# Values in self-attention: the low and high parts of three query tiles in one product of 129 columns, put together by VectorE

## The reference, cut to what matters

```python
q = (xq @ wq).reshape(b, sq, H, DH).transpose(0, 2, 1, 3)      # k and v likewise
scores = jnp.einsum('bhqd,bhkd->bhqk', q, k) / math.sqrt(DH)
attn = jax.nn.softmax(scores, axis=-1)
out = jnp.einsum('bhqk,bhkd->bhqd', attn, v)
```

## Time and profile before

| | |
|---|---|
| median of 3 runs | 1155.06 us (1154.7 to 1155.65) |
| the profiled execution's own time | 1157.49 us |
| its span | 1155.7 us |
| PE busy | 1075.3 us (93%), 12759 instructions |
| PE weight loads | 688.0 us (60%), 12766 |
| DVE busy | 820.2 us (71%), 1364 |
| ACT busy | 617.2 us (53%), 1123 |
| POOL busy | 699.0 us (60%), 640 |
| granted clock of PE, mean | 0.985 |

### The profile page before, as it was taken

The page is one execution under the profiler, slowest core; times in us unless marked ns, Lnnn a source line. Parts: engine busy times, 40 slices in busy tenths (PEclk is TensorE's granted clock), DMA queues, the critical chain, the costliest instruction groups (busy, mean ns, idle before and its releaser), DMA issues.

```text
span 1155.7 us, 30603 instructions
## 1 busy us (share of the span) xinstructions
PE 1075.3 (93%) x12759; PEld 688.0 (60%) x12766; DVE 820.2 (71%) x1364; ACT 617.2 (53%) x1123; POOL 699.0 (60%) x640
## 2 busy tenths in 40 slices
PE   6999998999999999999999998989899979999986
PEld 3555555565665665665656655567667656665654
DVE  5686876846756667867757567668778767797786
ACT  4456565545455455555555455544444543267677
POOL 6586887866566577867766665446436634434333
PEclk9899999999999999999999999999999999999997
DMA  9422021121120120220220222123533352000001
GB/s 310 115 56 56 3 56 31 27 56 30 30 56 16 42 57 1 57 56 2 57 56 2 56 56 75 31 61 70 143 72 77 73 160 71 1 1 10 15 14 38
DMA packets 35818, 63.52 MB, mean 55 GB/s; under 512 B 10985, under 2 KB 22689, under 8 KB 33441
## 3 DMA queue, kind: packets, MB, share of 16 engines
q1 hardware_dynamic: 34373, 60.90, 21.0%
q10 hardware_dynamic: 1308, 0.66, 0.2%
HBM read 20.62 MB, written 2.10 MB: 20 GB/s over the span
## 4 chain that ended last, share of the span: by engine, by line
PE 64%; DVE 20%; DMA 7%; ACT 4%; issue 3%; POOL 1%; SPq 1%; ACTq 0%; DVEq 0%; POOLq 0%
PE outs L827 9%; DVE neg_max L1909 8%; PE scores L901 8%; PE scores L902 7%; PE scores L962 5%; DMA head_operands<-neg_max_rows 4%; PE outs L976 4%; PE outs L923 3%; PE outs L925 3%; PE outs L924 3%; PE outs L799 3%; PE outs L839 3%; PE scores L799 2%; PE mixed L856 2%; PE scores L827 1%
## 5 line engine op out<-in xcount | busy, mean ns | idle before, releaser
L1619 POOL TENSOR_TENSOR exps_rest<-exps 128x1024 f16<-128x1024 f32 (+1 forms) x297 | 513.9, 1736 | 271.6 <-ACT exps L1262 269.6
L1262 ACT ACTIVATE exps<-scores 128x512 f32<-128x512 f32 (+1 forms) x576 | 328.8, 595 | 276.4 <-PE scores L902 258.6
L923 PE MATMUL outs<-values,exps 128*128 128x65 f16 (+1 forms) x2176 | 227.2, 193 | 5.4 <-DVE attn_out L1937 4.5
L901 PE MATMUL scores<-head_operands 128*128 128x512 f16 (+1 forms) x576 | 219.9, 382 | 11.2 <-DMA head_operands<-neg_max_rows 8.3
L924 PE MATMUL outs<-values,exps 128*128 128x64 f16 (+1 forms) x2176 | 227.1, 192 | 0.0
L925 PE MATMUL outs<-values,exps_rest 128*128 128x65 f16 (+1 forms) x2176 | 226.7, 195 | 0.0
L923 PEld LDWEIGHTS outs<-values,exps 128*128 128x128 bf16 (+1 forms) x2176 | 201.6, 98 | 40.4 <-issue 12.8
L902 PE MATMUL scores<-head_operands 128*128 128x512 f16 (+1 forms) x576 | 219.2, 381 | 0.0
L924 PEld LDWEIGHTS outs<-values,exps 128*128 128x128 bf16 (+1 forms) x2176 | 200.9, 98 | 21.9
L925 PEld LDWEIGHTS outs<-values,exps_rest 128*128 128x128 f16 (+1 forms) x2176 | 200.9, 97 | 0.0
L1909 DVE TENSOR_REDUCE neg_max<-mixed 128x1 f32<-128x1024 f32 x128 | 156.0, 1219 | 34.1 <-PE mixed L857 32.5
(11 more groups left out here) (220 smaller groups left out, 1885.0 us busy)
## 6 DMA issues: line engine op xcount, KB each, us to landing
head_operands<-qk_pairs SPq DMA_DIRECT2D x65, 256.0 KB, 3.2
head_operands<-qk_pairs SPq DMA_DIRECT2D x31, 512.0 KB, 5.7
head_operands<-qk_pairs SPq DMA_DIRECT2D x34, 128.0 KB, 2.5
stage<-in_L_xcond_ff_w_dram SPq DMA_DIRECT2D x3, 1024.0 KB, 5.6
residual<-in_x_dram SPq DMA_DIRECT2D x4, 512.0 KB, 9.9
stage<-in_L_ffn_w_dram SPq DMA_DIRECT2D x2, 1024.0 KB, 5.1
head_operands<-in_x_dram SPq DMA_DIRECT2D x1, 2048.0 KB, 8.3
out_dram<-head_operands SPq DMA_DIRECT2D x16, 128.0 KB, 1.7
```

What stands on the lines that cost most here:

```text
L901: mm(o, kb[:, KH, :], hb[:, QS, :], start=True, stop=False)
L923: mm(o, eb[:, sl], vb[:, DH:VW], start=(kt == 0 and q == 0), stop=False, skip_group_check=True)
L1262: A(E[0:a.ks, c % RING, j * HALF:(j + 1) * HALF], score_bank(a, c, j), ACT.Exp, scale=SCALE).then_inc(s.exps, 1)
L1619: G.tensor_tensor(R[0:a.ks, c % RING, 0:n], e, e.bitcast(BF16).rearrange("p (n two) -> p n two", two=2)[:, :, 1], ALU.subtract).then_inc(s ...
```

## The change

For query tiles 1 to 3 of a chunk, the products at L923 and L924 become one of 129 columns: low values, high values, ones. The bank `outs0` then holds 65 columns for query tile 0, which stays as it was, and 129 columns for each of the other three (452 of 512). The product with the rests stays at 65 columns and adds into the high part and the ones.

DVE then has five instructions in place of two: the reciprocal (of four values 129 columns apart), the multiply of tile 0 (64 columns, a tensor_scalar), the multiply of the three high parts (192 columns), the multiply of the three low parts (192 columns, into the new tile `low_parts`), and, after a wait for the latter, the sum of the two in SBUF (192 columns). The semaphore `emptied` rises after the multiply of the low parts, `summed` after the sum. PE's values steps of self-attention wait for `emptied` where they waited for `summed`; the "out" items still wait for `summed`. Cross-attention stays as it was.

```diff
+        lows = sb("low_parts", [P, 2, TPH - 1, DH], F32)
...
-                if gr == 0:
-                    pe.wait_ge(s.summed, CREDIT + 4 * g + h * 2 + half - (a.kt == 1))
+                if gr == 0 and ai == 0:
+                    at_least(pe, s.emptied, 4 * g + h * 2 + half)
+                elif gr == 0:
+                    pe.wait_ge(s.summed, CREDIT + 4 * g + h * 2 + half - 1)
...
                 for q in range(TPH):
-                    o = outs(a, c)[:, q * (DH + 1):(q + 1) * (DH + 1)]
+                    wide = ai == 0 and q > 0
+                    o = outs(a, c)[:, q * VW - DH:q * VW + DH + 1] if wide else outs(a, c)[:, q * (DH + 1):(q + 1) * (DH + 1)]
                     for j in range(a.kpc):
...
-                        mm(o, eb[:, sl], vb[:, DH:VW], start=(kt == 0 and q == 0), stop=False, skip_group_check=True)
-                        mm(o[:, 0:DH], eb[:, sl], vb[:, 0:DH], start=False, stop=False, skip_group_check=True)
-                        last = mm(o, R[0:a.ks, slot, sl], vb[:, DH:VW], start=False, stop=(kt == a.kt - 1),
+                        if wide:
+                            mm(o, eb[:, sl], vb[:, 0:VW], start=False, stop=False, skip_group_check=True)
+                        else:
+                            mm(o, eb[:, sl], vb[:, DH:VW], start=(kt == 0 and q == 0), stop=False, skip_group_check=True)
+                            mm(o[:, 0:DH], eb[:, sl], vb[:, 0:DH], start=False, stop=False, skip_group_check=True)
+                        last = mm(o[:, DH:VW] if wide else o, R[0:a.ks, slot, sl], vb[:, DH:VW], start=False, stop=(kt == a.kt - 1),
...
+                if ai == 0:
+                    n = 4 * g + 2 * h + half
+                    low = outs(a, c)[:, DH + 1:DH + 1 + 3 * VW].rearrange("p (t c) -> p t c", c=VW)
+                    dst = Osb[:, half * TPH:(half + 1) * TPH, h * DH:(h + 1) * DH]
+                    V.reciprocal(rden[:, half, :], outs(a, c)[:, DH:DH + 3 * VW + 1:VW]).then_inc(s.recip, 1)
+                    dve.wait_ge(s.recip, n + 1)
+                    V.tensor_scalar(dst[:, 0, :], outs(a, c)[:, 0:DH], rden[:, half, 0:1], None, ALU.mult)
+                    V.tensor_tensor(dst[:, 1:TPH, :], low[:, :, DH:2 * DH],
+                                    rden[:, half, 1:TPH].unsqueeze(2).to_broadcast([P, TPH - 1, DH]), ALU.mult)
+                    V.tensor_tensor(lows[:, n % 2, :, :], low[:, :, 0:DH],
+                                    rden[:, half, 1:TPH].unsqueeze(2).to_broadcast([P, TPH - 1, DH]),
+                                    ALU.mult).then_inc(s.emptied, 1)
+                    dve.wait_ge(s.emptied, n + 1)
+                    V.tensor_tensor(dst[:, 1:TPH, :], dst[:, 1:TPH, :], lows[:, n % 2, :, :], ALU.add).then_inc(s.summed, 1)
+                    return
```

More of the change, by code:

```diff
@@ L536, in __init__ @@
                 s.recip = sem(n + "_recip")
-                s.summed = sem(n + "_summed")
+                s.summed, s.emptied = sem(n + "_summed"), sem(n + "_emptied")
                 s.qk_hi, s.qk = sem(n + "_qk_hi"), sem(n + "_qk")
```

## The result

The changed kernel takes 1214.27 us (median of 3 runs, 1212.58 to 1215.41) against 1155.06: a ratio of 1.0507, with a 95% interval of 1.049 to 1.0525. It is 59.2 us slower. The forecast was 46.7 us slower, 1201.8 us, and the measured time lies 1.3 us above the upper end of the range. The direction and most of the places were right. One cost was not in the sum at all.

The account below looks back on a forecast made before the run. The prediction took a chain of waits alternating between PE and DVE as the bound. Terms 34.6 + 10.5 + 5.2 + 1.4 = 51.7 us, less 5 on PE, gave 46.7 us slower: 1201.8 us, range 1175 to 1213.

Parts of the forecast that it names:

- The sums after values 15: PE's transposes wait for these sums; DVE's sum, held up by POOL, was to cost 34.6 us over 16 units.
- 13 units x 2.48 = 32.2: After values 15, units 1 to 13: the sum ends 2.48 us later than the old multiply, 32.2 us together.
- The race of the two starts: After values 15, POOL's rest starts 0.05 us before DVE's sum; rival, sum first: 1179.8 us, chance 0.24.
- 2.48 - 0.79: After values 15, delay per unit: 2.48 us if POOL starts first, 0.79 if the sum does.
- DVE's durations: Multiplies of 192 at 356 ns, one tile's at 273, sum alone 0.36 us; sum ready 0.86 after the old multiply's start.
- After values 7: Sum ends 1.39 us later: 5.6 us in units 8 to 11, 4.9 in units 0 to 3, hidden elsewhere.
- After values 11: PE waits for the bank 0.40 us longer in units 4 to 15 and unit 1: 5.2 us.
- One of the rivals: Dearer still: DVE's rest after values 11 behind POOL in units 8 to 11, or values 7 unhidden; 1213 us, chance 0.08.
- After values 3: DVE's idle 1.8 us or more covers the 1.4 us delay; only unit 0 pays 1.4 us.
- PE: Values steps: one 129-column product replaces two, saving 5.4 ns each, 8.3 us in all, 5 us on the chain.
- The 81 ns: Rival for PE's wide product: the page's price makes it dearer than the two replaced; some 1225 us, chance 0.01.
- PE's wait before the transposes: PE's total wait for DVE there, 7.9 us before the change, was to be near 40 us.

Follow-up runs that it names:

- idle products: Changed kernel plus ten 512-column products before PE's wait for the sums after values 15, units 1 to 7, 12, 13: 1201.97 us, both times run.
- narrow products: Changed kernel with DVE's five instructions on the old 65- and 64-column products, three tiles' result doubled: 1218.92 us, ratio 1.0556.
- measured alone: Kernel before with the 129-column products only, low parts of three tiles left out of the result: 1152.65 us, ratio 0.9968.
- race lost everywhere: Changed kernel with one more 64-column multiply before the sums after values 15 in units 8 to 11: 1224.89 us, ratio 1.0609.
- tile 0 last: Changed kernel with tile 0's multiply moved behind those of three tiles, just before the sum: 1188.09 us, ratio 1.0277.

## Why the prediction was wrong

The ruler splits the loss of the profiled executions in four. In the middle is what the forecast's terms give for each part, at right the changed kernel and the one with idle products (its second profile, with nine lost units), each minus before. Parts end at the reciprocal after values 15.

| part of the span | forecast | after | idle products |
|---|---|---|---|
| to unit 0's last sum | 2.2 | 2.4 | 2.7 |
| from there to unit 13's | 40.3 | 47.1 | 32.5 |
| from there to unit 15's | 3.5 | 6.7 | 5.1 |
| behind it, with cross-attention | 0.8 | -1.1 | -5.0 |
| sum | 46.8 | 55.1 | 35.3 |

In the second row both measured numbers are 1.6 us too small for what the change costs: between values 3 and 7 of unit 7 the profile before is longer than all the others by about that much.

- **The step that failed** is "The sums after values 15", in "13 units x 2.48 = 32.2", which prices PE's longer wait by its length and nothing else. The length was right (2.39 us in unit 4). What it left out is that PE's clock, at 1.00 from unit 1 to unit 13 before, falls to 0.50 behind each of the nine waits of 3 us: 14.6 us over eight laps and 1.6 behind unit 13, some 16 us in the profiles compared here, 10 between the medians of the two kernels run side by side. The kernel before had PE idle for at most 0.8 us at this place. But one part of its trace did show the price, and I hadn't read it, unit 14, by windows:

```profile
714.00:717.00 3.00, 1.28 (x25) 0.68 (x21) 3.00 (x4) 0.52 (x1) 2.15 (x1) 0.97 0.47 111
717.00:718.00 1.00, 1.00 (x17) 0.78 (x16) 1.00 (x2) 0.00 (x0) 0.00 (x0) 0.50 1.08 376
718.00:719.00 1.00, 1.00 (x16) 0.67 (x13) 0.60 (x3) 0.00 (x0) 0.00 (x0) 0.50 0.91 321
```

  PE has 1.28 us of work in 3 us, and then works at 0.50. A forecast that makes PE idle for 3 us once a unit has to ask what such a place costs.
- **The race of the two starts** was rightly named as the hinge, but it is not one answer for all units. I had POOL first by 0.05 us in 13 units. It was in nine; in units 8 to 11 the sum was first by 0.04. The step took the reciprocal's place from before's rows, right behind DVE's maximum; in these four units the maximum is over by then, and the reciprocal starts 0.10 us sooner against POOL. Each of those saved 2.48 - 0.79 = 1.69, together 6.8 us, so this error went the other way and hid part of the first. With nine lost units the forecast for unit 0 to 13 is 33.5 us, and the kernel with idle products, which has nine and no low clock, shows 32.5 (34.1 with the 1.6 us of unit 7 added). A single execution doesn't settle the count: of the four profiles with wide products and this order of instructions three have nine, and one, with idle products, has 11; the one on narrow products has ten.
- **DVE's durations** were right: 348 ns for 356 forecast, 284 for 273, 0.36 for the sum alone, 1.06 us from the reciprocal to the sum.
- **After values 7**: 1.39 us forecast in units 8 to 11. There the ruler grows by 1.24 between values 7 and 11, the wide products' gain included. In units 0 to 3 it grows by 0.85 to 1.28, where 1.1 to 1.4 was forecast. Hidden in units 4 to 7, 12 and 13, as forecast, but not in unit 14 (1.8 us) and unit 15 (0.3).
- **After values 11**: 0.40 forecast, with 0.10 off for the products; units 4 to 7, 12 and 13 have +0.31 or +0.32, but unit 1 has +0.74 and units 8 to 11 have +0.53 to +0.83. One of the rivals had a delay in units 8 to 11 at this place; I did not trace what it is. **After values 3**: hidden, as forecast, but for unit 0, where 1.4 was forecast and the ruler grows by 1.38 to values 7.
- **PE**: 5 us forecast, 3.7 measured alone. The 81 ns of the Trainium skill, "TensorE: Matmul & The Clock Gate", section "Back-to-back issue gap", did not show: the trace has 57.7 ns from a product of 129 columns to the next. With the rests' product behind it that makes 86.9 ns, where three products took 92.4: 5.5 saved for the 5.4 forecast.
- **PE's wait before the transposes**: forecast near 40 us, 35.6 with nine units lost and 42.7 with 13.

Not explained: 55.1 us is the difference of two executions, 59.2 that of the medians. The last part of the table differs by 4 us between the two kernels, though nothing in it was changed; I have not traced that.

## What to carry to other kernels

Price a longer wait of TensorE twice, once by its length and once by what the clock does behind it: here a wait that went from 0.5 to 3 us cost its 2.4 us and, wherever the clock fell behind it, another 1.2 to 2.9. An instruction that reads two tensors in SBUF is cheap by its size and dear by its neighbour on POOL, so put what decides who starts first (an instruction's place, or what it stands behind, 0.1 us) into the plan, or use a form with one operand in PSUM. And a lag that one engine can absorb at three of four places is still paid in full at the one that the chain goes through.

## What the runs showed of the hardware

- TensorE's granted clock fell to 0.50 behind waits of 2.96 us, nine times of nine in the changed kernel and 12 of 13 with the race lost everywhere. What spared the one is open. Behind waits of 1.15 to 1.18 us (unit 5 with tile 0 last, unit 8 of the changed kernel) the transposes still took 0.63. In unit 15 it also fell behind shorter waits (1.61 us in the changed kernel, with another 0.87 us of idle time just ahead). With some 2.2 us of idle products in the wait it stayed at 1.00, nine times of nine in two profiles.
- A sum of 192 elements in SBUF takes 0.34 to 0.36 us if it starts 0.04 us ahead of POOL's instruction and 2.04 if it starts 0.06 behind it; POOL loses 0.15 to 0.18 us in the first case (tile 0 last; the changed kernel). This is the exclusive lock that the Trainium skill describes in "SBUF — State Buffer", section "SBUF: two separate sides", and the trace agrees; the trace adds how small a margin decides, and that it changes sign between units of one execution with what the instruction ahead of the sums on DVE does.
- With one operand in PSUM and one in SBUF the same arithmetic was not held up once in 192 instructions of 64 elements (278 ns each).
- Products of 64 or 65 columns start 30 ns apart and from the start of one of 129 to the next start it is 57.7: joining two products of 65 and 64 columns (61.6) saves the start of one, not its columns.
